# Feed-forward stage of a fused cross-attention block: statistics of the next block's tiles between the second half's products, each turn ahead of the second layer of the same number

## The reference

```
h3 = _ln(x, n3_g, n3_b)                      # mean and variance over 320 features
proj = h3 @ ff_w1 + ff_b1                    # 320 -> 2560
a, g = jnp.split(proj, 2, axis=-1)           # 1280 each
ff = a * jax.nn.gelu(g, approximate=False) @ ff_w2 + ff_b2    # 1280 -> 320
return ff + x
```

## Time and profile before

| | |
|---|---|
| median of 3 runs | 1368.8 us (1367.3 to 1371.93) |
| the profiled execution | 1369.08 us, its span 1367.2 us |
| feed-forward phase in the span | 1008.0 to the end |
| a first layer of 20 units | 46.96 us |
| from the end of a first layer to the start of the next | 24.39 to 24.49 us, four times |
| granted clock of TensorE, whole span | 0.991 |
| PE, DVE, ACT, POOL busy, whole span | 96%, 61%, 50%, 28% |

### The profile page before, as it was taken

How to read it: one execution, slowest core, us unless ns; L and a number is a source line. 1 busy time by engine, 2 the same in 40 slices (tenths; PEclk the granted TensorE clock), 3 DMA queues, 4 the chain that set the end, 5 groups by cost and what they waited for, 6 DMA issues and landing times. The chain is left out here.

```text
span 1367.2 us, 35359 instructions
## 1 busy us (share of the span) xinstructions
PE 1306.9 (96%) x13364; PEld 1215.0 (89%) x13364; DVE 828.1 (61%) x1728; ACT 678.3 (50%) x1558; POOL 382.6 (28%) x545
## 2 busy tenths in 40 slices
PE   5899789999999999999999999999889999999999
PEld 4799669889899889899889898988679999999999
DVE  5445367777777777777767777777674425242421
ACT  5555336556566556556556556555464131313131
POOL 5431222212222221221221221221076333333341
PEclk9999799999999999999999999999999999999999
DMA  4667454444444545545444444433302101010000
GB/s 130 212 227 253 152 151 145 132 129 142 137 133 139 158 139 156 158 137 157 144 138 146 135 126 143 150 117 91 80 27 73 49 2 48 0 46 2 24 1 25
DMA packets 121669, 155.60 MB, mean 114 GB/s; under 512 B 25012, under 2 KB 115372, under 8 KB 121516
## 3 DMA queue, kind: packets, MB, share of 16 engines
q1 hardware_dynamic: 121516, 153.52, 36.8%
HBM read 62.98 MB, written 28.93 MB: 67 GB/s over the span
## 5 line engine op out<-in xcount | busy, mean ns | idle before, releaser
L1362 ACT ACTIVATE probs<-expin 120x400 f32<-120x400 f32 (+2 forms) x640 | 304.9, 502 | 159.6 <-PE expin L701 151.4
L1036 DVE TENSOR_REDUCE neg_max<-score 100x2 f32<-100x722 f32 x320 | 291.1, 910 | 83.2 <-PE score L675 74.6
L701 PE MATMUL expin<-qs,ks 128*120 128x200 f32 (+2 forms) x1280 | 228.7, 277 | 8.4 <-PEq L1639 4.5
L701 PEld LDWEIGHTS expin<-qs,ks 128*120 128x120 f32 (+2 forms) x1280 | 185.9, 179 | 29.8 <-issue 10.2
L675 PE MATMUL score<-ks,qs 128*100 128x362 f32 x640 | 168.7, 345 | 6.0 <-DVE neg_max L1036 4.1
L2420 DVE SCALAR_TENSOR_TENSOR hidden<-ps_a,b_cols,gelu 128x320 f32<-128x320 f32 x100 | 55.0, 550 | 163.4 <-PE ps_a L2344 158.8
L1549 POOL TENSOR_TENSOR var_eps<-mv,eps 100x1 f32<-100x1 f32 x32 | 6.1, 191 | 421.4 <-DVE mv L1104 421.4
L2582 POOL TENSOR_TENSOR hid_lo<-hidden,hid_hi 128x320 fp32r<-128x320 f32 x100 | 89.2, 893 | 120.5 <-ACT hid_hi L2490 120.3
L2502 ACT ACTIVATE gelu<-ps_g,b_cols 128x320 f32<-128x320 f32 x100 | 52.8, 528 | 134.2 <-PE ps_g L2344 134.1
L125 DVE TENSOR_REDUCE neg_max<-score 100x10 f32<-100x1000 f32 x62 | 74.4, 1200 | 58.5 <-PE score L118 58.5
L724 PE MATMUL attn<-probs,vc 120*17 120x100 f32 (+1 forms) x3840 | 101.9, 250 | 0.1
(11 more groups left out here) (201 smaller groups left out, 2951.1 us busy)
## 6 DMA issues: line engine op xcount, KB each, us to landing
ks<-kc_parts SPq DMA_DIRECT2D x192, 181.0 KB, 2.7
qk_dram<-qk_parts SPq DMA_DIRECT2D x32, 500.0 KB, 5.0
qs<-q_parts SPq DMA_DIRECT2D x192, 75.0 KB
ks<-qk_dram SPq DMA_DIRECT2D x96, 125.0 KB
ctx_raw<-in_ctxT SPq DMA_DIRECT2D x64, 180.5 KB
ks<-kc_parts SPq DMA_DIRECT2D x96, 90.5 KB, 2.2
qs<-qk_dram SPq DMA_DIRECT2D x64, 125.0 KB
v_dram<-v_rows SPq DMA_DIRECT2D x32, 132.8 KB
```

Of the source, the lines that this page charges most:

```text
L701: mm = pe.matmul(dst, ks[a][u][:, c, j0:j0 + n], qs[a][u][:, :, q_slot(c) if a == 2 else c, :], start=True, stop=True)
L1036: ins = nc.vector.tensor_reduce(dst, src, AX_X, ALU.max, negate=True)
L1362: nc.scalar.activation(probs[e % NPT][0:n, :], expin[e % 2][0:n, 0:HG * N], ACT.Exp, scale=SCALE)\
```

## The change

Three engines get another order; no computation is added or taken away.

- PE: in every block the turn of tile i of the next block stands ahead of the second layer of tile i, not behind it. The first turn so follows directly on the last unit of the first layer.
- DVE: the statistics of the next block's tiles 0 to 4 follow the hidden features 12 to 16, `normalise` of tile 0 follows hidden feature 17 and that of tile 1 hidden feature 18 (a new function `prepare`). In `next_tiles` only `split_low`, the normalising of tiles 2 to 4 and the results are left, and the result of tile i comes behind `split_low` of tile i and `normalise` of tile i+2.
- POOL: the inverse deviations follow the remainders 13 to 17. In block 0, `xb` is made in units 6 to 10, so that SP can issue the loads of block 1's tiles in those units too.

```
         for i in range(TT):
-            second_layer(t, i)
-            turn_tile(t + 1, i)
+            turn_tile(t + 1, i)
+            second_layer(t, i)
...
+    def prepare(t, n):
+
+        if FT + 2 <= n < FT + 2 + TT:
+            statistics(t + 1, n - FT - 2)
+        if n in (NU - 3, NU - 2):
+            normalise(t + 1, n - NU + 3)
+
     def hidden_features(t):
         for n in range(NU):
             hidden_feature(t, n)
+            prepare(t, n)
...
     def next_tiles(t):
         for i in range(TT):
-            statistics(t + 1, i)
-        for i in range(2):
-            normalise(t + 1, i)
-        for i in range(TT):
-            result(t, i)
             split_low(t + 1, i)
             if i + 2 < TT:
                 normalise(t + 1, i + 2)
+            result(t, i)
...
-    def front(t):
-        for i in range(TT):
-            inverse_deviation(t, i)
+    def add_biases(t):
         pool.wait_ge(y_made, at(t, y_made, 0))
         for i in range(TT):
             add_bias(t, i)
...
+    def block_of(t):
         for n in range(NU):
             low_hidden_of(t, n)
+            if FT + 3 <= n < FT + 3 + TT:
+                inverse_deviation(t + 1, n - FT - 3)
+        add_biases(t + 1)
...
-        if FT <= n < FT + TT:
-            add_bias(0, n - FT)
-    front(1)
+        elif 6 <= n < 6 + TT:
+            add_bias(0, n - 6)
+        elif FT + 3 <= n < FT + 3 + TT:
+            inverse_deviation(1, n - FT - 3)
+    add_biases(1)
```

More of the change, by code:

```diff
@@ L2368, in _ @@
             for i in range(TT):
+                turn_tile(1, i)
                 second_layer(0, i)
-                turn_tile(1, i)
             with pe.Fori(1, NF - 1) as t:
@@ L2471, in _ @@
                     w2_low(n - FT)
+                prepare(0, n)
             next_tiles(0)
@@ L2475, in _ @@
                 next_tiles(t)
-            hidden_features(NF - 1)
+            for n in range(NU):
+                hidden_feature(NF - 1, n)
             for i in range(TT):
@@ L2583, in low_hidden_of @@
                                         ALU.subtract).then_inc(hid_lo_made, 1)
-            def low_hidden(t):
+            def block_of(t):
                 for n in range(NU):
                     low_hidden_of(t, n)
+                    if FT + 3 <= n < FT + 3 + TT:
+                        inverse_deviation(t + 1, n - FT - 3)
+                add_biases(t + 1)
             nc.gpsimd.memset(neg_half[:], -0.5).then_inc(constants_set, 1)
@@ L2601, in _ @@
                     inverse_deviation(0, EARLY + 1)
-                if FT <= n < FT + TT:
-                    add_bias(0, n - FT)
-            front(1)
+                elif 6 <= n < 6 + TT:
[3 more added lines that the diff above has]
+            add_biases(1)
             with pool.Fori(1, NF - 1) as t:
-                low_hidden(t)
-                front(t + 1)
-            low_hidden(NF - 1)
+                block_of(t)
+            for n in range(NU):
+                low_hidden_of(NF - 1, n)
 _P = "L0_xattn_"
```

## The result

| | before | changed |
|---|---|---|
| median of 20 runs | 1369.92 us (1366.34 to 1375.8) | 1366.64 us (1364.02 to 1369.6) |
| profiled execution, its span | 1369.08, 1367.2 us | 1365.24, 1363.4 us |

The ratio is 0.9977, 95% interval 0.9967 to 0.9986: 0.23% faster, where the prediction's sum gave 0.24% (3.3 us). The interval excludes no change, and the size stays inside the bound of 0.3%. The median of before lies 1.1 us above that of its first three runs, and that of the changed kernel 1.1 us above the forecast of 1365.5, so the difference of the medians is 3.3 us.

What follows compares the result with a forecast made beforehand. PE's products bound the first layers; at four boundaries PE waits for DVE's `h`. Losses of 0.85 + 0.85 + 0.84 + 0.75 = 3.29 us, less 0 cost, give 1365.8 profiled, 1365.5 median; range 1363.8 to 1368.0, widened to 1368.7.

Steps and rivals of the forecast that it cites:

- What bounds the boundary, and the sum: At four block boundaries PE waits for DVE's `h` and restarts slowly; 3.29 us lost, all won back.
- the restarts: Slow turns of PE after its boundary waits: 4 x (0.52 - 0.33) = 0.76 us of the loss.
- the waits: PE's turns waiting for `h` at the boundaries of blocks 0 to 3: 2.9 - 0.3 = 2.6 us.
- A turn directly behind a first-layer unit: PE's turn 0 straight after unit 19: 0.33 us taken, 0.52 at most, which would keep back 0.76 us.
- The wait of 0.3 us for `h` in block 0's units: PE's fifth wait for `h`, inside block 0's units: about 0.3 us, left alone by the change.
- DVE in units 12 to 16: Moved statistics fit DVE's idle 1.8 us per unit with 0.9 to spare, PE wanting features two units on; no cost.
- Units 17 and 18: Moved normalisings on DVE: `h` of tile 0 done at E(17) + 2.2, 2.5 us before PE needs it; no cost.
- Block 0, the loads in w2's time: Block 1's tile loads issued while w2 lands: cost taken as 0, at most 0.2 us kept.
- Rival A: The wait moves: DVE and POOL obstruct each other in the second half, PE waits there instead; 1368.8 us, chance 0.09.
- Rival B: Turn 0 loses its second-layer cover, late `h` stops PE; up to 17.6 us more, 1386.4 us; chance 0.05.

Runs made afterwards that it cites:

- dve_two_more: Changed kernel with two more bn_stats behind each moved statistics (units 12 to 16 of blocks 0 to 3): 1366.43 us, ratio to before 0.9973.
- dve_four_more: Changed kernel with four more bn_stats behind each moved statistics: 1366.72 us, ratio to before 0.9988.
- bias_late: Changed kernel with the bias of block 0 (`xb`) back in units 10 to 14: 1366.48 us, ratio to before 0.9984.
- late_h: Changed kernel with the normalisings of tiles 0 and 1 both behind unit 19: 1383.01 us, ratio to before 1.0097.
- turns_only: Kernel before with only PE's order changed, each turn ahead of the second layer of the same number: 1396.68 us, ratio to before 1.0197.

## Why the prediction was right, point by point

- **What bounds the boundary, and the sum.** Right. The loss was 3.29 us in the sum and 3.3 in the stretches after; the median moved by 3.3, with 1.9 to 4.5 in its interval. Two small slips changed nothing: the restarts (0.76) and the waits (2.6) add up to 3.36 and not to 3.29, and the low end of the forecast's own range, 1365.5 less 1.5, is 1364.0 and not 1363.8. All four boundaries came to 23.64 or 23.65, the price worked out from tiles 1 to 4.
- **A turn directly behind a first-layer unit.** Taken at its lower bound, 0.33; the chain has 0.33. The 0.76 us held for the upper bound weren't needed. The wait of 0.3 us for `h` in block 0's units, which the prediction expected to stay, is absent from this profile. It is absent from just those three of the nine in which PE began the phase at the lower clock, and the other six have it.
- **DVE in units 12 to 16.** No cost, right; idle time was to fall to about 1.1 us and fell to 1.18 in the loop. For block 0 the working left out the pieces of w2 that DVE splits in the same units: three hidden features there have only 0.38 or 0.39 us of idle time ahead of them (before 1.0 us), not 1.1 (that of unit 14 stands below). It cost nothing, but with less to spare than was claimed. dve_two_more and dve_four_more show that the cover was of the kind claimed: DVE's own idle first, then two units of PE.

```profile
1044.62 0.55 DVE L2420 SCALAR_TENSOR_TENSOR hidden<-ps_a,b_cols,gelu 128x320 f32<-128x320 f32 x1 [0.38 <-PE ps_a L2344]
```

- **Units 17 and 18.** `h` of tile 0 was put at E(17) + 2.2 and 2.5 us in hand; it came at E(17) + 1.83 (unit 17 ended at 1122.22) with 2.85 in hand. The 0.35 us that I had added for the loop's wait values don't exist as an extra: the distance from a hidden feature to the next instruction, 0.47, holds them already. The error was on the safe side.
- **Block 0, the loads in w2's time.** Taken as 0, right. The copies of w2 waited 0.57 us for the DMA, as 0.55 before, and w2 landed in 7.4 us. Of the five loads, the three now issued while it was landing took 6.0, 4.1 and 3.2 us and the other two 2.2 each, so that the median rose from 2.2 to 3.2. The small loads waited and the large one didn't. The Trainium skill's rule that the prediction cited for it (DMA: Bandwidth & Descriptors, section Queues, rings and completion order: descriptors are consumed in ring order) agrees with these times. But bias_late shows that the loads needn't have moved.
- **Rival A.** Didn't happen in the change. Its mechanism exists (0.6 us in late_h) where POOL's remainder is under way. Behind unit 17 the remainder ended at E(17) + 0.69, as computed, but `centred` began at E(17) + 0.50, since the 0.35 us didn't exist; the two overlapped by 0.2 us, and `centred` still took its 0.54. POOL paid instead: its `var_eps`, begun beside `centred`, took 0.44 us for 0.19, which nothing waited for.
- **Rival B.** Didn't happen; turns_only made it happen, and its price was wrong: 17.6 us over before were worked out, 27.9 measured. The wait was right (5.06); what was missing is PE at half clock for 6.5 us after it. In late_h the expectation of 8.7 us over the changed kernel met 16.4: 0.6 us more wait in each boundary (2.4), and in three of them the clock (4.7 by the stretches); the 0.6 us that are left are within scatter.
- **What the change consists of.** The prediction treated turn order and moved statistics as one. They aren't: the statistics carry the whole gain, and the turn order carries all of the risk.

## What to carry to other kernels

A wait of the engine that sets the time is removed by having its operand earlier, and the place for that work is where the other engines idle under a full stretch of that engine; how much fits there follows from their idle time per unit and from the depth of the buffers, two units here. Putting the consumer earlier as well gained nothing that the times show once the operand was early, and it takes away the cover that would hide the operand if it were late. When a late operand is priced for TensorE, the wait is only the first part: at 2.6 us the half clock behind it had already added 1.5 to 1.65 us in three cases of four, at 5 us it added 2.7.

## What the runs showed of the hardware

- TensorE's granted clock after a wait, in this kernel: behind 0.66 us or less at the boundaries of before it stayed at 1.00; behind 2.58 us (late_h) it fell in three cases of four, to 0.74 or 0.75 over the next 6.5 us; behind 5.0 us (turns_only) it was 0.53 to 0.55 over the next 6.5 us, all four times. At 1.2 GHz a product of 320 columns took 0.27 us in place of 0.147. Behind the 1.8 us at the start of the feed-forward phase, where PE had worked with gaps before, it fell in three of nine profiles and cost some 0.6 us.
- A DVE instruction with two inputs in SBUF that met POOL's remainder, begun 0.1 us before, ended 0.35 us after it: 1.15 us for 0.55 (late_h). bn_stats, with one input, kept its 0.46 to 0.49 in all profiles, 0.49 where a remainder ran beside it (bias_late, 1043.33).
- Loads of 160 KB issued on the same queue while one of 1600 KB was landing landed 0.4 us or more behind it: 6.0, 4.1 and 3.2 us in the changed kernel in place of 2.2. The large one took 7.4 to 8.6 us in the six profiles with such loads behind it and 7.9 to 8.1 in the three without, so no slowing beyond that spread is seen.
